# Softmax shifts brought to theta's rows by four small transfers per image instead of VectorE's transposes and products

## The reference

```python
theta = einsum('bchw,kc->bkhw', x, theta_w)            # 32 channels, 1024 pixels n
phi   = pool2(einsum('bchw,kc->bkhw', x, phi_w))       # 32 channels, 256 pooled pixels m
beta  = softmax(einsum('bnk,bkm->bnm', theta, phi), axis=-1)
g     = pool2(einsum('bchw,kc->bkhw', x, g_w))         # 128 channels, 256 pooled pixels
o_in  = einsum('bcm,bnm->bcn', g, beta)
y     = gamma * einsum('bchw,kc->bkhw', o_in, o_w) + x
out   = y + einsum('fc,bchw->bfhw', toeplitz(filter), y)   # 27 taps round the 256 channels
```

## Time and profile before

| | |
|---|---|
| median of three runs | 272.98 us (272.94 to 273.77) |
| profiled execution, span of its instructions | 271.3 us |
| TensorE matmuls | 265.4 us busy, 98% |
| TensorE weight loads | 211.8 us, 78% |
| VectorE | 245.9 us, 91% |
| ScalarE | 243.2 us, 90% |
| GpSimd | 149.6 us, 55% |
| granted TensorE clock | 0.998 of full speed |
| DMA traffic | 44.57 MB, 164 GB/s in the mean |

### The profile page before, as it was taken

The page is one execution under the profiler, slowest core; times in us unless marked ns, Lnnn a source line. Parts: engine busy times, 40 slices in busy tenths (PEclk is TensorE's granted clock), DMA queues, the critical chain, the costliest instruction groups (busy, mean ns, idle before and its releaser), DMA issues.

```text
span 271.3 us, 4464 instructions
## 1 busy us (share of the span) xinstructions
PE 265.4 (98%) x1196; PEld 211.8 (78%) x1196; DVE 245.9 (91%) x456; ACT 243.2 (90%) x533; POOL 149.6 (55%) x79
## 2 busy tenths in 40 slices
PE   7999999999999999999999999999999999999994
PEld 3576778888888888888888888888887888888873
DVE  4998999999999999999999999999999999999953
ACT  4999999999999999998999999999999989998772
POOL 1585747574565747546673764667466475745100
PEclk9999999999999999999999999999999999999999
DMA  7978085582847657284673828467283855317044
GB/s 198 270 208 212 23 234 169 175 223 81 193 142 225 180 170 182 88 218 149 203 201 144 180 79 246 157 197 206 98 182 124 234 169 172 77 71 178 1 157 155
DMA packets 17380, 44.57 MB, mean 164 GB/s; under 512 B 2654, under 2 KB 3578, under 8 KB 16122
## 3 DMA queue, kind: packets, MB, share of 16 engines
q1 hardware_dynamic: 16682, 44.00, 56.4%
q10 hardware_dynamic: 688, 0.46, 0.5%
HBM read 17.45 MB, written 16.78 MB: 126 GB/s over the span
## 4 chain that ended last, share of the span: by engine, by line
PE 94%; DVE 2%; DMA 2%; ACT 0%; issue 0%; SPq 0%
PE psY L1009 10%; PE psY L988 8%; PE psY L990 7%; PE psY L989 7%; PE psV L1128 6%; PE psY L1112 6%; PE psY L1128 5%; PE psV L1112 5%; PE psV L988 3%; PE psV L990 3%; PE psV L989 3%; PE psX L1066 3%; PE psV L1096 3%; PE psV L1133 3%; PE psZ L1066 3%; PE psY L1118 3%
## 5 line engine op out<-in xcount | busy, mean ns | idle before, releaser
L457 POOL TENSOR_TENSOR prob_lo<-prob,prob_hi 128x1024 fp32r<-128x1024 f32 x30 | 72.1, 2404 | 59.7 <-ACT prob L537 32.5
L450 POOL TENSOR_TENSOR x_lo<-x_raw,x_hi 128x1024 fp32r<-128x1024 f32 x30 | 72.0, 2399 | 35.5 <-ACT x_hi L504 34.0
L504 ACT CAST x_hi<-x_raw 128x1024 fp32r<-128x1024 f32 x30 | 31.5, 1052 | 6.8 <-PE psY L1096 5.2
L526 ACT ACTIVATE psX<-psX,neg_max 128x256 f32<-128x256 f32 x60 | 26.7, 445 | 3.0 <-DVE neg_max L777 3.0
L526 ACT ACTIVATE psZ<-psZ,neg_max 128x256 f32<-128x256 f32 x60 | 27.4, 468 | 0.0
L709 DVE TENSOR_TENSOR thetaphi<-psY,thetaphi_rest 64x512 f32<-64x512 f32 x30 | 20.5, 682 | 3.8 <-ACT thetaphi_rest L508 3.1
L988 PE MATMUL psY<-x_hi,g_hi_w 128*128 128x512 f32 x56 | 22.2, 396 | 0.0
L990 PE MATMUL psY<-x_hi,g_lo_w 128*128 128x512 f32 x56 | 22.0, 393 | 0.0
L989 PE MATMUL psY<-x_lo,g_hi_w 128*128 128x512 f32 x56 | 22.0, 392 | 0.0
L715 DVE TENSOR_TENSOR theta_aug<-thetaphi,theta_aug 32x512 fp32r<-32x512 f32 x30 | 20.5, 683 | 0.9
L702 DVE TENSOR_REDUCE phi_pool<-thetaphi 32x128 f32<-32x512 f32 x30 | 20.2, 674 | 1.0
(11 more groups left out here) (189 smaller groups left out, 766.1 us busy)
## 6 DMA issues: line engine op xcount, KB each, us to landing
x_raw<-x SPq DMA_DIRECT2D x30, 512.0 KB, 5.1
out<-y SPq DMA_DIRECT2D x15, 1024.0 KB, 4.0
x_edge<-x_hi SPq DMA_DIRECT2D x64, 104.0 KB
x_edge<-x_lo SPq DMA_DIRECT2D x32, 104.0 KB
x_raw<-x SPq DMA_DIRECT2D x4, 256.0 KB, 4.5
out<-y SPq DMA_DIRECT2D x3, 256.0 KB, 2.1
band_rev<-ring SPq DMA_DIRECT2D x2, 128.0 KB, 6.9
out<-y ACTq DMA_DIRECT2D x1, 256.0 KB, 2.6
```

What stands on the lines that cost most here:

```text
L450: nc.gpsimd.tensor_tensor(x_lo[:, par, :, cols], x_raw[:, par, :, cols], x_hi[:, par, :, cols].bitcast(F32), ALU.subtract).then_inc(x_lo_r ...
L457: nc.gpsimd.tensor_tensor(prob_lo[:, h], prob[:, h], prob_hi[:, h].bitcast(F32), ALU.subtract).then_inc(prob_lo_ready, 1)
L504: nc.scalar.copy(x_hi[:, par, :, cols], x_raw[:, par, :, cols]).then_inc(x_hi_ready[h], 1)
L526: last = nc.scalar.activation(tiles[:, t, :], tiles[:, t, :], ACT.Exp, bias=neg_max[:, col:col + 1], accum_out=exp_sum[:, col:col + 1])
```

## The change

The first two images keep their way. From the third image on:
- `shifts` writes the high and the low parts to a new tile `shift_cols`, where the 4 columns of a half lie side by side.
- VectorE's `turn_shifts` and `spread_shifts` are gone.
- SyncE's `turn_shifts` issues four transfers for each image at the end of its iteration, two after the wait for the high parts and two after the wait for the low parts. Each reads 4 values from each of 128 partitions and writes them, one partition after another, into 512 columns of one row of `theta_aug`: 96 for the high part, 97 for the low part.
- So column n of a half now holds the shift of partition n // 4, tile n % 4. To match, `scores` takes every fourth column of theta as weights for tile t (columns t, t + 4, ...), and the pixel on partition p of tile t is 4 p + t.
- scoresT waits for the two transfers of its half (one semaphore for each half and part) and is 98 rows deep (`K_SUM`) instead of 112.

```diff
+    K_SUM = R_SHIFT + 2
+        shift_cols = sb("shift_cols", [P, 2, 2 * NT], F32R)
-        shift_turned = sem("shift_turned")
+        shift_landed = [[sem(f"shift_landed{h}{part}") for part in range(2)] for h in range(2)]
+        def from_third(per_image, i, par, within):
+            return upto(per_image, i, par, within) - 2 * per_image
@@ SyncE @@
+            def turn_shifts(i, par):
+
+                for part, ready in enumerate((shift_hi_ready, shift_parts_ready)):
+                    sp.wait_ge(ready, from_second(1, i, par, 1))
+                    for h in range(2):
+                        row = theta_aug[R_SHIFT + part:R_SHIFT + part + 1, par, h * HALF:(h + 1) * HALF]
+                        sp.dma_start(row.bitcast(F32), shift_cols[:, part, h * NT:(h + 1) * NT].bitcast(F32)).then_inc(shift_landed[h][part], 16)
...
                 if has_next(i, par):
                     x_edges(*following(i, par))
+                    turn_shifts(*following(i, par))
...
-                nc.vector.tensor_copy(shift_parts[:, 0:2 * NT, 0], shift_sum_ps).then_inc(shift_hi_ready, 1)
+                if is_second(i, par):
+                    high, low = shift_parts[:, 0:2 * NT, 0], shift_parts[:, 0:2 * NT, 1]
+                else:
+                    high, low = shift_cols[:, 0, :], shift_cols[:, 1, :]
+                nc.vector.tensor_copy(high, shift_sum_ps).then_inc(shift_hi_ready, 1)
                 dve.wait_ge(shift_hi_ready, from_second(1, i, par, 1))
-                nc.vector.tensor_tensor(shift_parts[:, 0:2 * NT, 1], shift_sum_ps, shift_parts[:, 0:2 * NT, 0].bitcast(F32),
+                nc.vector.tensor_tensor(low, shift_sum_ps, high.bitcast(F32),
                                         ALU.subtract).then_inc(shift_parts_ready, 1)
@@ VectorE @@
-            def turn_shifts(i, par):
-                parts = shift_parts[:, :, :].rearrange("p t s -> p (t s)").bitcast(F32)
-                dve.wait_ge(shift_parts_ready, from_second(1, i, par, 1))
-                for q in range(0, P, SQUARE):
-                    last = nc.vector.transpose(shift_turned_ps[0:SQUARE, q:q + SQUARE], parts[q:q + SQUARE, :])
-                last.then_inc(shift_turned, 1)
-
-            def spread_shifts(i, par, h):
-                ...
-                nc.vector.tensor_tensor(rows[:, tiles, :], row, own_rows(tiles), ALU.mult).then_inc(shift_rows_ready, 1)
...
                 shifts(ni, npar)
-                turn_shifts(ni, npar)
-                for h in range(2):
-                    spread_shifts(ni, npar, h)
@@ TensorE, scores @@
                 for t in range(NT):
-                    n0 = h * HALF + t * P
-                    last = nc.tensor.matmul(tiles[:, t, :], theta_aug[0:R_SHIFT, par, n0:n0 + P],
+                    if is_second(i, par):
+                        columns = theta_aug[0:R_SHIFT, par, h * HALF + t * P:h * HALF + (t + 1) * P]
+                    else:
+                        columns = theta_aug[0:R_SHIFT, par, h * HALF + t:h * HALF + t + NT * (P - 1) + 1:NT]
+                    last = nc.tensor.matmul(tiles[:, t, :], columns,
                                             phi_aug[0:R_SHIFT, par, :], start=True, stop=True)
@@ TensorE, scoresT @@
-                pe.wait_ge(shift_rows_ready, upto(2, i, par, h + 1))
+                if is_number(i) and i == 0:
+                    pe.wait_ge(shift_rows_ready, upto(2, i, par, h + 1))
+                else:
+                    for part in range(2):
+                        pe.wait_ge(shift_landed[h][part], 16 * from_third(1, i, par, 1))
+                rows = K_AUG if is_number(i) and i == 0 else K_SUM
                 for t in range(MT):
-                    last = nc.tensor.matmul(scores_ps[h][:, t, :], phi_aug[0:K_AUG, par, t * P:(t + 1) * P],
-                                            theta_aug[0:K_AUG, par, h * HALF:(h + 1) * HALF], start=True, stop=True)
+                    last = nc.tensor.matmul(scores_ps[h][:, t, :], phi_aug[0:rows, par, t * P:(t + 1) * P],
+                                            theta_aug[0:rows, par, h * HALF:(h + 1) * HALF], start=True, stop=True)
```

More of the change, by code:

```diff
@@ L123, in attention_then_channel_filter @@
         shift_ps = psZ[0:SHIFT_ROWS, 0, 0:P]
-        shift_turned_ps = psZ[:, 1, 4 * NT:4 * NT + P]
         ln_sum_ps = psZ[:, 1, 0:2 * NT]
@@ L798, in shift_rows @@
                 tiles = slice(h * NT, (h + 1) * NT)
-                nc.vector.tensor_tensor(rows[:, tiles, :], row, own_rows(tiles), ALU.mult).then_inc(shift_rows_ready, 1)
-            def turned(i, par):
-                return from_second(1, i, par, 0)
-            def turn_shifts(i, par):
-                parts = shift_parts[:, :, :].rearrange("p t s -> p (t s)").bitcast(F32)
-                dve.wait_ge(shift_parts_ready, from_second(1, i, par, 1))
-                for q in range(0, P, SQUARE):
-                    last = nc.vector.transpose(shift_turned_ps[0:SQUARE, q:q + SQUARE], parts[q:q + SQUARE, :])
-                last.then_inc(shift_turned, 1)
-            def spread_shifts(i, par, h):
[L813 to L816, removed]
                 nc.vector.tensor_tensor(rows[:, tiles, :], row, own_rows(tiles), ALU.mult).then_inc(shift_rows_ready, 1)
```

## The result

The changed kernel takes 301.38 us in the median of four runs (301.13 to 301.65), the kernel before 272.96: a ratio of 1.103, 95% interval 1.1005 to 1.1053. It is slower by 28.4 us, 2.03 us in each of the 14 images that the change touches. The granted TensorE clock is full in both, 0.998 before and 1.0 after, so it has no part in this. The forecast was 288.5 with a range of 278 to 304: right in sign and within the range, but short of the size by almost half.

The account below looks back on a forecast made before the run. TensorE's own work was taken as the 16.05 us period of an image. A stall of 14 x 1.1 + 0.1 = 15.5 us, all else 0, added to 272.98 gave 288.5 us, with an 8-in-10 range of 278 to 304.

Parts of the forecast that it names:

- What bounds the kernel: TensorE's own work is the 16.05 us period of an image; VectorE's freed 2.2 us becomes idle time, worth 0.
- The shifts can't come earlier: On VectorE, the high shifts stay at 111.48 and the low at 111.67 relative to TensorE's matmuls; gain counted 0.
- The wait: TensorE stands ahead of scoresT of half 0 until the third transfer lands: 1.1 us in each of 14 images.
- An issue: SyncE's issuing of one shift transfer, taken as 0.50 us with ends 0.39 and 0.75; two lie on the path.
- a landing: Time from the third shift transfer's issue to its landing, taken as 1.9 us with ends 1.4 and 2.6.
- the queue's waking: SyncE's queue reacting once the high shifts are ready, an allowance of 0.07 us.
- The restart: After standing at scoresT, TensorE's first weight load is bare ahead of its matmul: some 0.17 us more an image.
- The fourth transfer, the moved loads, the queue: On SyncE's queue, the last transfer costs 0.1 us in the last image only; later loads, store and edge copies cost 0.
- Strided weights: Scores matmuls load every fourth theta column: taken as 0; if bare before 8 matmuls, 1.5 us an image, 21 us.
- rival C: The forecast stall plus strided scores loads at half their bound, 0.75 us an image: 299 us; chance 0.12.
- the likeliest case: TensorE's stall at scoresT with strided loads free: 288.5 us, own range 281 to 296, chance 0.57.
- rival B: Slow shift transfers, issue 0.75 and landing 2.6 us, stall 2.3 us an image: 305 us; chance 0.22, from 297 up.

Follow-up runs that it names:

- transfers alone: The changed kernel with contiguous instead of strided weights in the scores matmuls, the four transfers kept: 292.03 us, ratio 1.069.
- the queue alone: The kernel before plus the four transfers on SyncE's queue, from a zero tile to an unread spare tile, VectorE still bringing the shifts: 272.82 us.
- the ScalarE control: The kernel before with only ScalarE's order changed, theta's high part and the theta and phi copy ahead of half 0's exponentials: 287.82 us, ratio 1.055.

## Why the prediction was right, and where it was short

- *What bounds the kernel*: right. VectorE's 2.2 us an image turned into 2.5 us of idle time and gave nothing. TensorE was the period, and everything that it lost was lost.
- *The shifts can't come earlier*: right, as far as the distance from the scores goes. In the trace before, the high shifts are done 5.86 us after the scores of half 0 (105.62 to 111.48); after, 6.19 us (114.58 to 120.77), longer by 0.33 us, about what the strided scores of half 1 take more (0.34).
- *The wait*: right in kind and place, 14 images, psX, released by a transfer. The sum was 1.1 us an image and the run with transfers alone measured 1.35. An issue took 0.60 us (taken: 0.50), a landing 2.0 (taken: 1.9), the queue's waking 0.03 (taken: 0.07). The first two were between their bounds. Two issues and a landing add 0.30 us to the path and the waking takes off 0.04: 0.26, which is the difference. The restart (taken: 0.17) shows only as the 0.1 us between the landing and the first weight load. The 2.0 us that the Trainium skill's "DMA: Bandwidth & Descriptors" gives as a fixed cost, in the section "Anatomy of one DMA — SWDGE (gpsimd) path", was a better price for a landing on SyncE's queue too than my 1.9, which was set from the stores.
- *The fourth transfer, the moved loads, the queue*: right, nothing (272.82 us with the queue alone).
- *Strided weights*: this step failed. I took 0, "the nearest row being the same load unstrided", and set the alternative as rival C with a chance of 0.12 and 10.5 us. It was 9.5 us, measured alone. The bounds were 0 and 21 us, and the sum took the lower one; the row nearest in form was not the row nearest in access. C's mechanism came, but not by its condition: a load already took 0.19 us where the matmuls stood 0.12 apart, and hid. At 0.31 us it no longer did, four in a row took 1.02 us instead of 0.66. The Trainium skill's rule on 16-byte lines, quoted in the prediction, named the exact step (four f32 values) and deserved more than a rival's 0.12.
- The outcome is the forecast's wait together with rival C, which had said 299. The own range of the likeliest case, 281 to 296, missed. The wide range of 278 to 304 holds 301.38 in part by luck: its upper end came from rival B, an issue of 0.75 and a landing of 2.6, and neither came.

## What to carry to other kernels

When the busiest engine has no gaps and does not wait for another engine, work taken from that other engine is worth nothing. A transfer of 2 KB that the busiest engine waits for cost here two microseconds from its issue plus every issue ahead of it (0.6 us each), so such a path is free only if the engine has that much other work to do in the meantime. A layout chosen so that a small transfer has contiguous pieces is paid by whoever reads it: weights taken from every fourth float32 loaded 0.12 us slower and no longer hid behind the 256-column matmuls, while every second float32 was free. In a schedule this tight, moving one stage by a microsecond to cover a wait moved the wait to another engine's work each time (three versions), so a cover has to be tried with a control that has the new order and not the change.

## What the runs showed of the hardware that was not expected

- Weight loads of 96 x 128 float32: 190 ns contiguous, 196 ns with a step of two, 312 ns with a step of four. Between 512-column matmuls 0.23 us apart the slow ones are hidden.
- A transfer of 2 KB in 128 pieces of 16 bytes into a single partition lands in 2.0 us (1.9 to 2.1), about as long as a store of 256 KB (2.1). Its issue, 0.60 us, is dearer than that of a 512 KB load, 0.385.
- A VectorE cast of 32 x 256 from on-chip memory to on-chip memory takes 0.28 us at its shortest, and up to 2.15 beside a GpSimd subtraction of 2.4 us in the ScalarE control: it ended only when GpSimd had. The instructions of L735 there (ns min/median/max):

```profile
L735 DVE CAST phi_aug<-phi_pool x28: 283/1148/2154, 38.9 to 262.8; 32x256 fp32r<-32x256 f32 x28
```

The Trainium skill, "SBUF — State Buffer", section "Who interferes with whom", says that a cast with both operands in on-chip memory can take a mode in which it and a GpSimd instruction exclude each other for a whole instruction, by order of issue. The rows agree: the first cast is issued at 124.12, 0.4 us after GpSimd's subtraction, and ends at 126.26, 0.14 after it.
